# Taking 550 waited pairs of one-row memsets out from behind GpSimd's indirect transfers

## What is computed

```python
x = x + _L0_gnn_ref(_layernorm(x), edge_index, ...)      # attention by exp(-leaky_relu), sum over edges
x = x + _L0_ffn_ref(_layernorm(x)[None], ...)[0]         # 32 experts, the best one of each node
x = x + _L1_gnn_ref(_layernorm(x), edge_attr_8, edge_attr_4, ...)
x = x + _L1_ffn_ref(_layernorm(x)[None], ...)[0]         # 6 experts of three layers, the best two
x = x + _L2_gnn_ref(_layernorm(x), src, dst, ...)        # 4 heads, softmax over the edges of a node
x = x + _L2_ffn_ref(_layernorm(x)[None], ...)[0]         # 8 experts, all
x = x + _L3_gnn_ref(_layernorm(x), ..., src, dst)        # 4 heads, softmax over the edges of a node
x = x + _L3_ffn_ref(_layernorm(x)[None], ...)[0]         # 8 experts of two layers, the best two
```

## Time and profile before

| | us |
|---|---|
| median of three runs | 4936.28 |
| span of the profiled execution | 4927.7 |
| TensorE busy | 3735.8 (76%) |
| VectorE busy | 3216.6 (65%) |
| GpSimd busy | 2811.3 (57%) |
| ScalarE busy | 2672.8 (54%) |

### The profile page before, as it was taken

The page is one execution under the profiler, slowest core; times in us unless marked ns, Lnnn a source line. Parts: engine busy times, 40 slices in busy tenths (PEclk is TensorE's granted clock), DMA queues, the critical chain, the costliest instruction groups (busy, mean ns, idle before and its releaser), DMA issues.

```text
span 4927.7 us, 75534 instructions
## 1 busy us (share of the span) xinstructions
PE 3735.8 (76%) x19152; PEld 2468.1 (50%) x19152; DVE 3216.6 (65%) x8314; ACT 2672.8 (54%) x8902; POOL 2811.3 (57%) x3741
## 2 busy tenths in 40 slices
PE   6878999644279999969577777778999956666564
PEld 2346666443134444558345555545656545555453
DVE  9976777442459999875668888743333446666743
ACT  6855777412168888844247777643233335665321
POOL 4667777777778888517247777530000057777064
PEclk9989999757589999989789899889999967777698
DMA  3023333443223333422446666610000033434424
GB/s 130 22 63 93 92 92 92 62 103 94 61 68 93 91 92 91 63 84 80 128 137 179 178 178 179 157 49 1 13 13 7 11 90 104 105 102 100 86 69 133
DMA packets 278831, 441.45 MB, mean 90 GB/s; under 512 B 114083, under 2 KB 192782, under 8 KB 278158
## 3 DMA queue, kind: packets, MB, share of 16 engines
q0 software_dynamic: 124624, 331.70, 26.8%
q1 hardware_dynamic: 147230, 98.37, 7.0%
q10 hardware_dynamic: 6560, 6.55, 0.4%
HBM read 368.84 MB, written 67.60 MB: 89 GB/s over the span
## 4 chain that ended last, share of the span: by engine, by line
PE 36%; POOL 23%; issue 16%; DVE 16%; DMA 4%; ACT 4%; DVEq 1%; POOLq 0%; SPq 0%; ACTq 0%
POOL bigt L1030 7%; PE PB L2011 7%; PE PB L3159 7%; POOL bigt L2659 5%; PE PB L3143 4%; POOL RECS L365 4%; POOL iotai L346 3%; PE PB L2021 2%; PE PB L2541 2%; PE PB L734 2%; DMA bigt<-YTAB,bigt 2%; DVE XNT L2934 1%; POOL OUTS L1716 1%; ACT XNT L2625 1%; PE PB L2033 1%
## 5 line engine op out<-in xcount | busy, mean ns | idle before, releaser
L2541 PE MATMUL PB<-XNT 128*128 128x260 f32 x1760 | 582.9, 468 | 24.2 <-DVE bigt L2513 20.4
L1983 POOL DMA_INDIRECT bigt<-YTAB,bigt x440 | 481.7, 1095 | 119.4 <-issue 118.6
L2659 POOL DMA_INDIRECT bigt<-ZTAB,DO x440 | 447.2, 1016 | 168.0 <-issue 120.9
L1030 POOL DMA_INDIRECT bigt<-HTAB,bigt x440 | 423.8, 963 | 157.8 <-issue 89.5
L365 POOL DMA_INDIRECT RECS<-bigt x391 | 390.5, 999 | 190.5 <-DVE bigt L713 109.5
L725 ACT ACTIVATE bigt<-bigt 128x128 f16<-128x128 f16 x1214 | 373.9, 388 | 141.2 <-DVE bigt L698 141.2
L2625 ACT ACTIVATE XNT<-bigt 128x65 f32<-128x65 f32 x1768 | 446.2, 336 | 0.0
L2541 PEld LDWEIGHTS PB<-XNT 128*128 128x128 f32 x1760 | 361.6, 227 | 82.6 <-DVE XNT L2421 24.7
L2659 POOL DMA_INDIRECT bigt<-KVTAB,DO x296 | 295.2, 997 | 186.5 <-DMA KVTAB<-bigt 83.0
L2011 PE MATMUL PB<-bigt 128*128 128x512 f32 x880 | 397.3, 593 | 3.0 <-DVE bigt L2199 3.0
L734 PE MATMUL PB<-bigt 128*128 128x440 f16 x1564 | 352.2, 354 | 28.0 <-ACT bigt L725 20.4
(11 more groups left out here) (491 smaller groups left out, 9673.3 us busy)
## 6 DMA issues: line engine op xcount, KB each, us to landing
bigt<-YTAB,bigt POOLq DMA_INDIRECT x552
bigt<-SRT SPq DMA_DIRECT2D x56, 128.0 KB, 2.7
OUTS<-bigt SPq DMA_DIRECT2D x56, 128.0 KB, 2.2
SRT<-bigt SPq DMA_DIRECT2D x11, 640.0 KB, 9.9
bigt<-HTAB,bigt POOLq DMA_INDIRECT x440, 2.8
bigt<-ZTAB,DO POOLq DMA_INDIRECT x440, 2.8
KVTAB<-bigt SPq DMA_DIRECT2D x25, 258.0 KB, 2.4
YTAB<-bigt SPq DMA_DIRECT2D x10, 640.0 KB, 10.5
```

Of the source, the lines that this page charges most:

```text
L1030: e.indirect_dma_start(out=Gt[:, g % GB, j, :], out_offset=None, in_=HTAB, in_offset=bass.IndirectOffsetOnAxis(ap=SO[:, g * G + j:g * G + ...
L1983: e.indirect_dma_start(out=Gt[:, g % GB, j, :], out_offset=None, in_=YTAB, in_offset=bass.IndirectOffsetOnAxis(ap=SO[:, g * G + j:g * G + ...
L2541: m = e.matmul(self.PV[n % len(self.PV)], self.OH[:, g % self.MB, j, :], self.msg[:, g % self.MB, j, :], start=(k == 0), stop=(k == self.H ...
L2659: e.indirect_dma_start(out=dst[:, j, :], out_offset=None, in_=table, in_offset=bass.IndirectOffsetOnAxis(ap=DO[:, g * G + j:g * G + j + 1] ...
```

## The change

All calls of `rest` go, the function with them, and the argument `run` of `gather_rows`. Nothing is put in their place; all transfers and their waits stay as they are and in the same order.

```diff
-        def rest(e):
-
-            for _ in range(2):
-                e.memset(iotai[0:1, :].bitcast(FP), 0.0).then_inc(Q.up(), 1)
-                e.wait_ge(*Q.now())
-
...
                     in_=ATTR[:, piece % 2, k, :], in_offset=None).then_inc(recs_out[piece % 2].sem, 16)
-                if n > 1 and c % 2:
-                    rest(e)
                 recs_next[0] = c + 1
...
                         ).then_inc(gathered.sem(g), 16)
-                        if (g * G + j) % 3 == 2:
-                            rest(e)
...
                             ).then_inc(fetched.sem(s), 16)
-                        rest(e)
                     return
...
                         in_=xs[:, t, :], in_offset=None).then_inc(rows_out.sem, 16)
-                    if t % 2:
-                        rest(e)
                 attr_scatters(e, 116)
...
-        def gather_rows(e, dst, table, n, landed, run=0):
+        def gather_rows(e, dst, table, n, landed):
...
                 ).then_inc(landed, 16)
-                if run and (g * G + j) % run == run - 1:
-                    rest(e)
...
-                    gather_rows(e, slot(g), KVTAB, n, kv_in.sem(n), 3)
+                    gather_rows(e, slot(g), KVTAB, n, kv_in.sem(n))
```

## The result

The changed kernel takes 4740.19 us (median of four runs, 4739.4 to 4740.72), the kernel before 4936.06 us beside it: ratio 0.9604, 95% interval 0.9593 to 0.9615. That is 196 us less, where 154 were forecast; it lies inside the range. Its span is 4738.5 us.

What follows compares the result with a forecast made beforehand. GpSimd's list was taken as full, the gain limited by how close TensorE (A, C, E) or VectorE (D) stood. 48 + 44 + 10 + 32 + 20 = 154 us; 4927.7 - 154 + 8.6 = 4782 us, range 4715 to 4840.

Steps and rivals of the forecast that it cites:

- A: Layer 0's edge loop, 440 gathers of HTAB: 48 us less, ends 25 and 77 us.
- B: Scatters and gathers around layer 0's experts: 44 us less, ends 35 and 48 us.
- C: Layer 1's experts: 10 us less, ends 3 and 38 us.
- D: Layer 2's attention, 440 gathers of KVTAB: 20 us less, ends 0 and 55 us.
- E: Layer 3's experts: 32 us less, ends 20 and 39 us.
- The rule on VectorE and GpSimd excluding each other: Attention: closer gathers would hold VectorE's line 2398 and D would gain nothing; weighed, but D's 20 us kept.
- a pause keeps the next transfer short: Rival: without the pair one transfer per former pair takes 1.83 us instead of 0.95, 5118 us in all; chance 0.03.

Runs made afterwards that it cites:

- Only_a: The kernel before with only the 146 pairs of layer 0's edge loop taken out: 4859.04 us, ratio 0.9845.
- a_three_gathers: The changed kernel without the fourth gather of each group in layer 0's edge loop, its rows taken from the third: 4667.45 us, ratio 0.9477.
- Experiment 6: The changed kernel with VectorE's reduce in layer 2's attention summing only 32 of each head's 64 numbers: 4679.74 us, ratio 0.949.

## Why the prediction was right, and where it was off

The time was forecast at 4782 us and is 4740, inside 4715 to 4840; "faster" had 0.95. By its steps:

- **A, 48 us forecast, 77 measured: the size of the term was wrong.** The step was "It stands still 34.4 us for the scores that need the gathered rows ... I take the 34.4 us and no more", after "From 420 to 930 us it is nearly full". It took idle time for all the room that TensorE had. GpSimd still sets A's pace, and 146 x 0.53 = 77 us came whole, as the high end had it "if TensorE's modelled busy time shrinks too". It did, from 181 to 168 ns a matmul, about half of it by more overlap. Only_a shows the 76 us alone, and a_three_gathers that 163 ns can be reached.
- **B, 44 us forecast, 46 and 43 measured: right**, with its parts. The first 30 pairs were covered (the wait grew from 5.69 to 13.90 us, 8 us where 13 were said), and the 25 gathers behind the RECS scatters (line 1747 before, 1734 in the changed kernel) begin 1143.5 - 962.07 = 181 us after the first SRT scatter, where 183 was said.
- **C, 10 us forecast, 24.5 measured: wrong in the same step as A.** "TensorE waits for gathers only 6.8 us in 150 us" was true, and its 138.17 busy us held more slack than the 11.83 idle ones. In the changed kernel it is 136.96 of 137 us busy and GpSimd waits for VectorE's L1660 behind it, so C has reached TensorE's pace: 165.1 us, not the 151.6 us that the whole price would give (189.6 less 55 x 0.69 = 38). The forecast named the bound rightly and its distance wrongly: a step "near 3.1" was said, and it is 2.86 us.
- **D, 20 us forecast, 11 measured: half.** I took all of VectorE's waits for KVTAB, 17.2 + 3.7, to be winnable. 10.8 us of them are still there, all in the first 75 us, where the gathers can't be ahead yet. Behind them VectorE never waits for a gather, and it is at 88% before and after; the rest of its idle time there is 28 us for TensorE's L2528 and 24 us of "issue". Experiment 6 took 59 us out of its list and 63 out of D. The page of the changed kernel doesn't show the 90% that I named.
- **E, 32 us forecast, 34.6 measured: right in size, not in its bound.** The forecast put TensorE's own step, 2.67 us, above GpSimd's 2.57 and named TensorE as the next limit. The step is 2.57 us and TensorE still waits 7.5 us for gathers, so GpSimd sets the pace; the 2.67 was worked out from TensorE's idle time alone, as in A and C.
- **The gathers didn't get longer.** Their means are 963 ns for HTAB before and 959 after, 997 and 973 for KVTAB, 1016 and 1015 for those of layer 3's attention. The medians are 954 and 953, 947 and 946, 946 and 946. The pauses did nothing for what follows them.
- **The rule on VectorE and GpSimd excluding each other was read from one side only.** The prediction looked whether VectorE's line 2398 is held. It is not, as the one-hot line takes 1209/1216/1257 ns in the changed kernel's 110 cases too. But GpSimd is held: the "long gathers" of the prediction are gathers that start while such a VectorE operation runs. The first line below is what VectorE did as the gather of the earlier trace rows began; the other two are a pair of the changed kernel.

```profile
4106.45 1.22 DVE L2398 TENSOR_TENSOR bigt<-iotab,DK 128x1024 bf16<-128x1024 bf16 x1
...
2644.70 1.22 DVE L2385 TENSOR_TENSOR bigt<-iotab,DK 128x1024 bf16<-128x1024 bf16 x1
2644.86 1.87 POOL L2646 DMA_INDIRECT bigt<-KVTAB,DO  x1 [0.30 <-issue]
```

Both gathers end 0.81 us after the VectorE operation ends. Counted over the trace of the kernel before, 64 of the 880 gathers of the two attentions start with more than 0.15 us of line 2398 still to run, and all 64 end 0.81 to 0.85 us after it. For all 86 gathers over 1.15 us a VectorE `tensor_tensor` with its inputs in SBUF runs during their first 0.15 us; the 637 gathers beside which none does take 1.04 us at most. The Trainium skill (SBUF — State Buffer, Who interferes with whom) says that a VectorE operation with two SBUF inputs and a GpSimd instruction that reads SBUF exclude each other, and the second of them blocks. The trace agrees, in these 64 cases with the gather as the one that waits, and shows no case where VectorE does. So the rival "a pause keeps the next transfer short" had the wrong reason for these lengths, and layer 3's mean is above A's because of its VectorE work. In D the gathers over 1.15 us fell from 34 to 14. Those left cost nothing, since GpSimd has slack there now; whether the 20 fewer gave a part of D's 11 us is not separated.

A and C were 43 us too small, B and E 4, D 9 too large, and 4 us were lost between the stretches: 35 us, which is the span's 189 against 154. The other 7 of the 42 us are no effect of the change: I carried 8.6 us from the profiled span to the median, and here the median lies 1.7 us above the span.

## What to carry to other kernels

When an engine issues transfers back to back at a fixed distance, what it has to wait for between them costs its whole price in every stretch where that engine sets the pace; work that nobody waits for can hide in the distance (0.08 us instead of 0.53). The idle time of the engine behind it can be less than what can be won: TensorE's busy time held overlap still to come, so compare busy time per matmul between a dense stretch and this one. VectorE's did not, and there the idle time was an upper bound. Price the second copy of a cost too: in D the first pair cost 11 us and the second 77. And where single transfers are long, look at what the other engines ran at that moment before blaming the transfers.

## What the runs showed of the hardware that was not expected

- On one of the chips two kernels without the pairs were 3.8% slower than the kernel with them, and on another one of the same two was 3.7% faster. That chip also ran the kernel before 7% slower (5279 against 4928 to 4936 us).
- Of the 0.53 us of a pair, only 0.08 was left once nobody waited and the memsets were half as wide: a memset of GpSimd of 0.14 us hides in the 0.30 us between two indirect transfers.
- An indirect gather that starts during VectorE's line 2398 (1.21 us, two inputs from SBUF) with over 0.15 us of it left ends 0.81 to 0.85 us after that line, in all 64 cases of the kernel before, and so takes up to 2.0 us instead of 0.95; VectorE's operation keeps its length.
- TensorE's busy time per matmul in the same loop was 181, 168 and 163 ns, in this order as the gathers came closer, with the clock at 0.96, 0.98 and 1.00; the first step is 7% for 2% of clock. The matmuls' own lengths were 195, 188 and 184 ns; the rest is overlap.
